# A one-core graph network kernel: attribute gathers in accumulating form, 52 of them moved ahead, and a hold by two groups on every edge gather

## What is computed

```
x = _layernorm(x + _L0_gnn_ref(...))   # two layers of attention over edges, with feed-forward parts
x = _layernorm(x + _L1_gnn_ref(...))   # one layer of attention by source, four heads of 64
x = _layernorm(x + _L2_gnn_ref(...))   # hypergraph convolution, twice: m = A x ; out = A^T m
x = _layernorm(x + _L3_gnn_ref(x, edge_attr_4, edge_attr_10, ...))

# _L3: message of an edge, then the sum over its target
src = node_in[edge_src]
h = silu(edge_len_emb @ fc_w1 / sqrt(10)) * SILU_NORM
messages = msg_ang(src, edge_attr) * (h @ fc_w2 / sqrt(64))
agg = segment_sum(messages, edge_dst) / sqrt(16)
```

## Time and profile before

| | |
|---|---|
| median of 3 runs | 5668.25 us (5663.96 to 5679.35) |
| profiled execution, its own time | 5646.56 us |
| span of the profile | 5645.4 us, 59886 instructions |
| busy: PE, DVE, ACT, POOL | 3618.7, 2869.4, 1858.3, 3438.4 us |
| mean granted TensorE clock | 0.81 |

### The profile page before, as it was taken

One profiled execution on the slowest core, in us unless ns is written; L12 is line 12 of the kernel. 1 busy time (PEld: TensorE's weight loads), 2 busy tenths in 40 slices (PEclk: granted clock), 3 DMA queues, 4 the chain that ended last, 5 costly groups with the idle time before them and its releaser, 6 DMA issues.

```text
span 5645.4 us, 59886 instructions
## 1 busy us (share of the span) xinstructions
PE 3618.7 (64%) x15291; PEld 2680.2 (47%) x15291; DVE 2869.4 (51%) x6725; ACT 1858.3 (33%) x5462; POOL 3438.4 (61%) x3085
## 2 busy tenths in 40 slices
PE   4554443667964444599794666621116999968887
PEld 3433232445653232366563444411005888767776
DVE  6465567886434454788532667622002322434445
ACT  1243344663333343577231111100001010146655
POOL 4466667888886666788887666677771000046664
PEclk8876677998986666799896888865558999979988
DMA  7688885663258888576424666621004878846665
GB/s 259 198 288 279 281 289 152 161 161 50 22 119 276 287 278 288 134 169 141 71 20 76 174 168 179 173 31 20 11 11 142 262 228 276 251 142 178 178 175 141
DMA packets 688351, 951.03 MB, mean 168 GB/s; under 512 B 230789, under 2 KB 479668, under 8 KB 687880
## 3 DMA queue, kind: packets, MB, share of 16 engines
q1 hardware_dynamic: 419634, 538.30, 31.0%
q0 software_dynamic: 251600, 385.84, 28.1%
q10 hardware_dynamic: 16774, 23.00, 1.2%
HBM read 727.03 MB, written 219.80 MB: 168 GB/s over the span
## 4 chain that ended last, share of the span: by engine, by line
issue 26%; PE 23%; POOL 19%; DVE 11%; another core or an unknown queue 10%; DMA 6%; SPq 3%; ACT 1%; DVEq 1%; ACTq 0%; POOLq 0%
PE bank L2650 10%; POOL arena L927 6%; POOL sc L950 6%; POOL ATT L964 6%; PE bank L2775 6%; PE bank L2772 4%; DMA ATT<-arena 3%; DMA sc<-arena 2%; SPq L620 2%; DVE arena L1376 2%; DVE arena L1746 2%; DVE arena L1466 2%; DVE arena L1352 1%; PE bank L2490 1%
## 5 line engine op out<-in xcount | busy, mean ns | idle before, releaser
L927 POOL DMA_INDIRECT arena<-KVT,arena x832 | 801.4, 963 | 480.5 <-issue 280.3
L2490 PE MATMUL bank<-arena 128*128 128x264 f32 x1664 | 598.5, 512 | 659.8 <-issue 366.1
L927 POOL DMA_INDIRECT arena<-YT,arena x416 | 405.7, 975 | 932.6 <-DMA YT<-arena 721.6
L2490 PEld LDWEIGHTS bank<-arena 128*128 128x128 f32 x1664 | 384.9, 248 | 872.8 <-issue 663.6
L964 POOL DMA_INDIRECT ATT<-arena x391 | 644.1, 1647 | 125.1 <-issue 110.0
L950 POOL DMA_INDIRECT sc<-arena x391 | 641.6, 1641 | 125.1 <-issue 111.5
L1466 DVE TENSOR_TENSOR arena<-arena,bank 128x256 f32<-128x256 f32 x832 | 297.5, 413 | 564.5 <-remote 360.9
L927 POOL DMA_INDIRECT arena<-X1T,arena x416 | 412.0, 990 | 243.5 <-issue 126.1
L2447 PE MATMUL bank<-arena 128*128 128x273 f32 x1664 | 455.1, 412 | 141.5 <-DVE arena L1525 94.5
L2631 PE MATMUL bank<-arena 128*128 128x261 f32 x832 | 315.8, 530 | 293.9 <-DVE arena L1376 158.2
L980 POOL DMA_INDIRECT arena<-ATTR,arena x416 | 416.4, 1001 | 139.7 <-issue 139.7
(11 more groups left out here) (333 smaller groups left out, 6661.0 us busy)
## 6 DMA issues: line engine op xcount, KB each, us to landing
VE<-arena SPq DMA_DIRECT2D x208, 512.0 KB
arena<-VE SPq DMA_DIRECT2D x208, 512.0 KB
left<-ATT SPq DMA_DIRECT2D x250, 320.0 KB
left<-AM SPq DMA_DIRECT2D x250, 320.0 KB
ATT<-arena POOLq DMA_DIRECT2D x25, 1600.0 KB, 6.6
arena<-LOCT SPq DMA_DIRECT2D x312, 128.0 KB
arena<-ATT SPq DMA_DIRECT2D x75, 384.0 KB
AM<-arena SPq DMA_DIRECT2D x100, 256.0 KB
```

The costliest lines, as they stand in the source:

```text
L927: GP.indirect_dma_start(out=ring[:, i % n, k, :], out_offset=None, in_=table, in_offset=bass.IndirectOffsetOnAxis(ap=idx[:, 4 * i + k:4 * ...
L2490: mm = P.matmul(b_[:, 0:264], OHQ[:, i % 3, k * 128:(k + 1) * 128], QS[:, i % 4, k, :], start=True, stop=True)
```

## The change

Three things are changed.

- The attribute gathers get `bounds_check` and `compute_op=ALU.add`: the rows are added to what stands in PA[:, c, 2:6]. Therefore DVE sets these columns to 0 in the preparation, behind the copy of the edge numbers.
- The first 52 of the 416 are issued ahead of the l1 gathers, behind the scatters into ATT; the other 364 stay behind the l1 gathers.
- In `gather`, which serves the loops k0, k1, l1 and l3, POOL waits ahead of group i (from the third on) until group i - 2 of the same loop has landed.

```
+EARLY = 52
...
         def gather(name, i, table, width, idx, ring_o):
             n = GATHERS[name]
             ring = view(ring_o, n, 4, width)
+            if i >= 2:
+                GP.wait_ge(*gathered(name, i - 2))
             for k in range(4):
                 GP.indirect_dma_start(
...
+        def add_attributes(cols):
+            for c in cols:
+                GP.indirect_dma_start(
+                    out=PA[:, c, 2:6], out_offset=None, in_=ATTR,
+                    in_offset=bass.IndirectOffsetOnAxis(ap=PA[:, c, 0:1].bitcast(I), axis=0), bounds_check=R1 - 1,
+                    compute_op=ALU.add).then_inc(attr_back.sem, 16)
+
+        GP.wait_ge(*attr_out(1))
+        add_attributes(range(EARLY))
         GP.wait_ge(*index_made("l1", 1))
         GP.wait_ge(*acc_clear("l1", 1))
...
             gather("l1", i, X1T, 72, idst, o_ring)
 
-        GP.wait_ge(*attr_out(1))
-        for c in range(T):
-            GP.indirect_dma_start(
-                out=PA[:, c, 2:6], out_offset=None, in_=ATTR,
-                in_offset=bass.IndirectOffsetOnAxis(ap=PA[:, c, 0:1].bitcast(I), axis=0)).then_inc(attr_back.sem, 16)
+        add_attributes(range(EARLY, T))
         GP.wait_ge(*acc_clear("l3", 1))
...
         d.then(V.tensor_copy(PA[:, :, 0].bitcast(I), PA[:, :, 2]))
+        d.mark(V.memset(PA[:, :, 2:6], 0.0))
```

## The result

The changed kernel takes 5287.85 us (median of 4 runs, 5282.66 to 5292.56), the kernel before 5670.16 us on the same chip (4 runs, 5663.96 to 5679.35). The ratio is 0.9324, with a 95% interval of 0.9308 to 0.934: 6.8% faster. The forecast was 5305 us.

The account below looks back on a forecast made before the run. Plain attribute gathers on POOL were taken to hold up PE's semaphore increments, idling the other engines for 556 us. 5646.6 - 378 + 15 + 1 = 5285 us, plus 21.7 for timed runs: 5305 us; range 5180 to 5690.

Parts of the forecast that it names:

- The form of the attribute gathers: Attribute gathers with addition and bound take 1.97 us each, like scatters, not 1.337; PE's news is then not held up.
- The 52 early gathers: On POOL between the last scatter and l1: they lie on the path and cost 102 us (70 at 1.337).
- The end of l1: Last l1 gather at 3802, open groups take 38 us more: l1 ends at 3840, 18 us earlier than before.
- The 25 windows: Layernorm, projection, first product part after l1: 72 us plus 28, ending at 3940 instead of 4318, 378 us gained.
- The products: Hops after the windows: 660 us, PE-bound, plus 15 us contention from 364 gathers; end 4615, last gather 4519.
- the "DVE blocks DMA" trap: Skill rule against the products' cover: GpSimd can't write descriptors during VectorE two-port operations, so gathers there would be longer.
- The hold: POOL's wait by two groups in k0, k1, l1, l3: taken as 0 us, both ends kept.
- The bound upwards: Late landings under the hold: k0's first 1.28 us of delay free, each us beyond costs 104 us a loop.
- the bound downwards: If the hold thins bursts and PE's news flows, k0, k1 and l1 each win up to 133 us.
- The form changes nothing: First rival: attribute gathers stay at 1.337 us and PE's news stays starved; 5675 us, chance 0.13.
- The second rival: Attribute gathers slower, PE starved all the same until the last gather at 4519; 5930 us, chance 0.14.
- the third: Gathers become the bound beside the products, last landing at 4709; 5400 us, chance 0.11 (gathers or DMA).

Follow-up runs that it names:

- The form undone: Changed kernel with attribute gathers in the plain form (no bounds_check, no compute_op), early gathers and hold kept: 5676.87 us against 5664.04 for the kernel before.
- the fills on the kernel before: Kernel before with two small GpSimd fills, each waited for, ahead of each plain attribute gather: 5167.27 us against 5639.33, ratio 0.9154.
- the kernel with none early: Changed kernel with EARLY = 0, all 416 attribute gathers behind the l1 gathers: 5211.53 us against 5664.04 for the kernel before, ratio 0.9206.

## Why the prediction was right, and where it holds

**What bounded the kernel** was read rightly: PE's increments, held up while POOL issues plain gathers. The form undone brought the 484 us of standstill back, the fills on the kernel before took it away with nothing else changed, and the recorded rises show the delay itself. Three readings on the way were off without harm. From ScalarE's end to PE's start 0.14 us pass in the earlier trace rows (3957.10 to 3957.24), not 0.5. From 4284.85 to 4318 PE's records are 127 and not 139 (that is the count from 4257 on), so a window takes 3.1 us there, not 2.9. And the longest wait of 2.0 us in the scatter stretch is that of one line of ScalarE; another line there waited for PE as long as in the standstill:

```profile
ACT arena L2126 <- PE bank L2360: 116.6, 29, 23.2
```

But these waits have PE as their named releaser, so PE was working until then, and the recorded rises bear the comparison out: 0.014 us in the scatter stages, 14.5 beside the plain attribute gathers.

**How near, and how far by luck.** For the profiled execution 5285 us was worked out, and 5282.66 was measured; the 17 us between forecast and median are the 21.7 us by which the timed runs before stood above their profiled one, against 5.2 us after. Errors of the stages cancelled (below): l1 began 3 us early, the windows ended 11 us late, the products cost 14 us less. The stated range of 5180 to 5690 would have held "nothing changes" too; what bears the mechanism out is the stage times and the experiments.

**The form of the attribute gathers.** Taken: 1.97 us, from the scatters. Measured: 1.98 (718.6 us from 3805.7 to 4524.3, over 363), median 1.549 against the scatters' 1.563. The choice of row was right because the arguments set the price, not the direction; that the addition and not the bound makes it was not foreseen.

**The 52 early gathers.** Taken: 102 us, l1 from 3148. Measured: 99 us, from 3144.7, and 76 us of the end time by the kernel with none early.

**The end of l1**: taken 3840, measured 3847. **The 25 windows**: taken 100 us, measured 104, so the products began at 3951 where 3940 was forecast; of the 378 us of gain 367 came.

**The products.** Taken: 660 us and 15 of contention, first YT gather at 4615. Measured: 661, 4612.3, so contention cost 1 us where 15 were taken, which made up for the 11 of the step before. The last attribute gather starts at 4524.3, 88 us ahead (taken: 96), and POOL then waits:

```profile
4524.29 1.55 POOL L974 DMA_INDIRECT arena<-ATTR,arena  x1 [0.30 <-issue]
4612.33 1.00 POOL L930 DMA_INDIRECT arena<-YT,arena  x1 [86.49 <-DMA YT<-arena]
```

The Trainium skill, "SBUF — State Buffer", the "DVE blocks DMA" trap, spoke for longer gathers beside VectorE's operations in a two-port mode. The trace shows little of it: with DVE busy 220 of 661 us their median is still 1.549 us and their mean 1.588 (660.6 us over 416), 0.04 above the median. Which of DVE's operations there ran in such a mode no row tells, so this does not test the page's rule itself.

**The hold.** Taken: 0, measured 0 on the first chip. The bound upwards was right in kind: the slack of k0 was worked out from this kind of chip, and where the loops run at POOL's own pace there is none. Of the bound downwards (the hold thins the bursts and PE's news flows again) nothing came: k0 and k1 take 627.6 us each from first to last gather, where they took 624.0 and 623.6, and PE's increments are as late in them as before.

**The rivals.** "The form changes nothing" was worked out at 5675 us; the plain form with everything else changed measured 5676.87. That this comes within 2 us is partly luck: the first YT gather moved by 27 us (4978.5 to 5005.4) where 6 were worked out, and the 21.7 us added on top are not in this run. The second rival fell with the copies' waits (none over 4.6 us), the third with POOL's 86 us of waiting. It came back elsewhere: with none early, the gathers are just the bound (some 20 us), and on the 4790 chip too.

**What the prediction did not see** is that all of this differs from chip to chip. On a 4790 chip there is no standstill to remove. What is left of the change is its costs: the hold 79 us (4793.80 to 4872.41), then form and early gathers together 92 us (to 4964.42; l1's first gather moves from 2937.2 to 3033.4, 96 us):

```profile
L930 POOL DMA_INDIRECT arena<-X1T,arena x416: 940/944/1470, 3033.4 to 3582.2; - x139
```

Nothing in the profile before tells how another chip behaves, but the prediction did name both costs: the 102 us of the early gathers, and the slack beyond which the hold costs.

**What stays open.** Why the increments are late on some chips is not shown; nor whether what helps is the time between gathers or the engine's own wait in it (the fills are each waited for). The pace from which it sets in lies between 1.36 us (starved) and 1.84 us (not), no closer. That fewer gathers under way would also help was not tested where it counts, but the trace speaks against a backlog of data: beside the plain attribute gathers of the kernel before, the 16 packets of 128 bytes of a gather have ended 0.97 us after it in the median, less than one gather's pace, and sooner than the 2.1 us on a 4790 chip or with the fills, where nothing is late.

One more thing in the traces wants an explanation. In the starved stretch few rises of any semaphore are recorded: 770 in 540 us (3710 to 4250), against 13326 in 535 us (3490 to 4025) of the kernel with the hold on a 4790 chip. `attr_back`, which each gather raises by 16, has 625 of them for 404 gathers, against 6508 for 408. And of the 115 intervals over 0.5 us between the rises that engines make there, 74 are within 0.02 us of a multiple of 0.7 us. So the number of increments that a gather makes, and not only its time, may be what counts; no run varied it.

Spacing the gathers inside the edge loops, where the increments are late too, was not tried. On a 4790 chip the fills alone were not run; with early gathers and hold they gave 4948.23 (one run), 16 us less than the changed kernel.

## What to carry to other kernels

When every engine but one has work and stands still, compare two stretches in which that one engine is equally busy and ask what differs: here it was the pace of GpSimd's indirect DMAs, and 0.5 to 0.6 us more between them gave 7 to 8.5% on the chips that stood still. Separate the parts of such a change before keeping it: the simplest version, plain gathers with a filler between, had a lower ratio than the one with three edits (0.9154 against 0.9324); the early gathers cost some 70 us, and the hold cost nothing on one kind of chip and 79 us on the other. When a wait has no named releaser, compare the time at which its semaphore rose with the end of the instruction that raises it. And run the kernel before on more than one chip, because a change that removes a standstill that only some chips have can be 7% faster on one and 4% slower on the next.

## What the runs showed of the hardware

- The same program takes 5664 us on one chip and 4793 us on another, each steady within 0.6%. The attribute stretch shows it best: PE busy 90 of 556 us, or 500 of 547, beside the same gathers. 854 of the 871 us lie in the stages with plain indirect gathers; stages with accumulating scatters take the same time on both.
- An indirect gather of 128 rows costs GpSimd 0.944 us; with a bound 1.010; with bound and addition 1.549. The gap behind it is 0.3 us in each case (median).
- Beside gathers 1.34 us apart TensorE's semaphore increments come 14.5 us late on a 5660 chip (median of the recorded ones; 15.9 at 1.33 us in the plain form, 11.4 at 1.36 with the bound); at 1.84 and 1.98 us apart, 0.014 us. VectorE's are late as well, up to 10.0 us.
- In the edge loops of such a chip, whose gathers come in bursts of four 1.25 us apart, they are 1.0 to 2.1 us late in the median and up to 13.5 (kernel before); on a 4790 chip 0.014 us.
- Two fills of 128x144 on GpSimd, each with a semaphore wait, add 0.5 us between gathers; a register load adds nothing that can be seen.
